# Feed-forward on four PSUM banks with the attention's tail and the narrow attention's head beside its products, and the wide attention's probability sums taken for four heads at once

## The reference

```python
# L0: 20 heads of 64 ("wide")
x = cross_attention(layer_norm(x, g1, be1), layer_norm(x, g1, be1), wq1, wk1, wv1, wo1, bo1) + x
x = cross_attention(layer_norm(x, g2, be2), context, wq2, wk2, wv2, wo2, bo2) + x
h = einsum('bne,ef->bnf', layer_norm(x, g3, be3), w1) + b1      # 320 -> 2 * 1280
a, gate = h[..., :1280], h[..., 1280:]
x = einsum('bnf,fe->bne', a * gelu(gate), w2) + b2 + x
# L1: the same block with 20 heads of 16 ("narrow") and the exact gelu
# L2: attention over 2 x 16 context tokens with two gates, + x
# L3: cross attention with 20 heads of 16, + x
# inside each attention
attn = softmax(q @ k.T * scale);  out = (attn @ v) @ wo + bo
```

## Time and profile before

| | |
|---|---|
| median of 3 runs | 3481.67 us (3481.03 to 3483.08) |
| the profiled execution, its own time | 3482.07 us |
| its span | 3480.3 us |
| granted TensorE clock, mean | 0.985 |
| PE busy | 3284.0 us (94%) |
| DVE, ACT, POOL busy | 1760.0 (51%), 1505.8 (43%), 672.0 (19%) us |
| the chain that ended last | PE 86%, ACT 6%, DVE 5%, issue 2% |

### The profile page before, as it was taken

The page is one execution under the profiler, slowest core; times in us unless marked ns, Lnnn a source line. Parts: engine busy times, 40 slices in busy tenths (PEclk is TensorE's granted clock), DMA queues, the critical chain, the costliest instruction groups (busy, mean ns, idle before and its releaser), DMA issues.

```text
span 3480.3 us, 39327 instructions
## 1 busy us (share of the span) xinstructions
PE 3284.0 (94%) x15478; PEld 1478.6 (42%) x15478; DVE 1760.0 (51%) x2728; ACT 1505.8 (43%) x2023; POOL 672.0 (19%) x420
## 2 busy tenths in 40 slices
PE   7999999999999999998999899999997999989997
PEld 3434344443434343434454344444433455643443
DVE  2645455454545455562223666777771221656774
ACT  3544444444454545451111555666652111326664
POOL 2433334333334343340000000000000000000000
PEclk9999999999999999999999999999999999989999
DMA  3000000000100000002000000000003000000000
GB/s 109 20 16 19 17 16 19 22 15 22 32 16 19 16 22 13 16 7 59 0 1 25 1 1 1 22 9 7 1 1 83 0 1 22 3 5 6 5 1 31
DMA packets 43558, 60.54 MB, mean 17 GB/s; under 512 B 7408, under 2 KB 31216, under 8 KB 43376
## 3 DMA queue, kind: packets, MB, share of 16 engines
q1 hardware_dynamic: 43376, 58.02, 5.8%
HBM read 55.39 MB, written 2.62 MB: 17 GB/s over the span
## 4 chain that ended last, share of the span: by engine, by line
PE 86%; ACT 6%; DVE 5%; issue 2%; DMA 0%; POOL 0%; SPq 0%; ACTq 0%; DVEq 0%; POOLq 0%
PE bank L548 8%; PE bank L465 8%; PE bank L1027 6%; PE bank L670 5%; PE bank L350 5%; PE bank L606 4%; PE bank L1463 4%; PE bank L960 4%; PE bank L1465 4%; PE bank L1143 3%; PE bank L609 3%; PE bank L642 3%; PE bank L1466 2%; PE bank L1080 2%; PE bank L1168 2%; DVE heads L985 2%
## 5 line engine op out<-in xcount | busy, mean ns | idle before, releaser
L498 DVE TENSOR_REDUCE heads<-bank 128x2 f32<-128x1024 f32 x320 | 392.4, 1226 | 673.7 <-PE bank L487 673.7
L985 DVE TENSOR_REDUCE heads<-bank 128x1 f32<-128x512 f32 x960 | 597.9, 683 | 237.2 <-PE bank L973 236.4
L521 ACT ACTIVATE probs<-bank 128x1024 f32<-128x1024 f32 x320 | 327.7, 1024 | 130.1 <-PE bank L474 129.9
L534 POOL TENSOR_TENSOR heads<-heads,probs 128x1024 f32<-128x1024 f32 x160 | 377.1, 2357 | 12.5
L530 POOL TENSOR_TENSOR heads<-probs 128x1024 f32<-128x1024 f32 x80 | 192.4, 2405 | 931.9 <-ACT probs L521 931.9
L465 PE MATMUL bank<-heads 64*128 64x512 f32 x1280 | 335.7, 602 | 0.1
L960 PE MATMUL bank<-heads 32*128 32x512 f32 x1920 | 296.5, 628 | 25.7 <-ACT weights L998 14.9
L548 PE MATMUL bank<-probs,values 128*64 128x512 f32 x1280 | 292.3, 598 | 9.3 <-ACT heads L617 4.9
L577 DVE RECIPROCAL rec<-ox 128x128 f32<-128x128 f32 x320 | 270.2, 907 | 8.0 <-ACT ox L570 8.0
L998 ACT ACTIVATE weights<-bank 128x1024 f32<-128x1024 f32 x238 | 230.6, 1021 | 100.2 <-PE bank L960 99.6
L1487 ACT ACTIVATE probs<-bank,b_col 128x512 f32<-128x512 f32 x80 | 55.0, 687 | 455.3 <-PE bank L1466 455.3
(11 more groups left out here) (199 smaller groups left out, 4725.2 us busy)
## 6 DMA issues: line engine op xcount, KB each, us to landing
heads<-in_wqk SPq DMA_DIRECT2D x40, 320.0 KB, 2.9
heads<-in_wqk SPq DMA_DIRECT2D x40, 256.0 KB, 2.6
ctx_in<-in_ctx SPq DMA_DIRECT2D x12, 384.0 KB, 3.7
weights<-in_L_xattn_wo SPq DMA_DIRECT2D x2, 1600.0 KB, 11.7
x_res<-in_x SPq DMA_DIRECT2D x4, 640.0 KB, 12.3
out<-x_res SPq DMA_DIRECT2D x1, 2560.0 KB, 8.7
weights<-in_L_xattn_w_ff SPq DMA_DIRECT2D x1, 1600.0 KB, 12.3
weights<-in_L_xattn_ff_w SPq DMA_DIRECT2D x1, 1600.0 KB, 14.2
```

Of the source, the lines that this page charges most:

```text
L498: nc.vector.tensor_reduce(v["negm"][:, U % 2, qb, :].rearrange("p (g k) -> p g k", g=2)[:, :, 0], M.ROWS[:, :, :], AX.X, ALU.max, negate=T ...
L521: nc.scalar.activation(v["probs"][:, kb, :, :], M.COLS[kb % 2][:, :, :], ACT.Exp, scale=float(r.work[n][0].prm["dh"]) ** -0.5).then_inc(r. ...
L534: nc.gpsimd.tensor_tensor(ps, ps, pr[:, k, :, :], ALU.add).then_inc(r.sem("part"), 1)
L985: nc.vector.tensor_reduce(v["negm"][:, tile, qb, 32 * h + at:32 * h + at + 1], r.bank_of(item, m)[:, :], AX.X, ALU.max, negate=True).then_ ...
```

## The change

1. *Wide run, denominators.* `den` is taken only in odd steps, for the pair of this step and the one before: four products with 32 columns of `ones` each instead of two with 64. The result has the four heads in four strips of 32 partitions. DVE takes four reciprocals per two steps (in the even step after), and ACT then spreads them: a copy of all 512 columns and four copies of 32 partitions, from strip to strip, to give one divisor for the even pair (`rec`) and one for the odd pair (`rec_odd`). DVE divides two pairs in the next odd step.
2. *Wide run, turns.* y moves from u = 1 to 4 to u = 2 to 5, V2 from u = 5 and 6 to u = 0 and 1. In the last batch u = 7 gets T0 to T2 of the feed-forward's first batch. The round after the last batch is gone: the y tiles of batch 7 stand behind the products j = 1 to 4 of the feed-forward.
3. *Feed-forward.* Gate in banks 2 and 3, linear half in 0 and 1, y in 0 and 1, input in 6 and 7. For odd j the pair on 64 rows comes first, ahead of the full products, so that the pairs of two j stand next to each other. The third input transposition moves behind the first tile of y. The weights come in two blocks in the order in which they are used, the first during the attention.
4. *Narrow run.* Its head stands between the pieces of the last batch's output product in s2 (`MEET`), its tail behind the products j = 0 to 3 of s5 (`TAIL`). Weight tiles and probability slots get other places in SBUF.

The core of the diff:

```diff
                 if u in (1, 2, 3, 4) and old:            # WideRun.step_items, wide_pe
-                    items += [(f"y{u - 1}", n - 1)]
+                if u in (2, 3, 4, 5) and old:
+                    items += [(f"y{u - 2}", n - 1)]
-                if u in (5, 6) and now:
-                    items += [(f"V2_{2 * u - 10}", n), (f"V2_{2 * u - 9}", n)]
+                if u in (0, 1) and now:
+                    items += [(f"V2_{2 * u}", n), (f"V2_{2 * u + 1}", n)]
...
-            for g in range(2):                           # w_den_pe
-                last = nc.tensor.matmul(r.bank_of(item, n)[64 * g:64 * g + 64, :], M.ones[:, :], v["psum"][:, U % 2, g, :], start=True, stop=True)
+            for e in range(2):
+                for g in range(2):
+                    at = 64 * g + 32 * e
+                    last = nc.tensor.matmul(r.bank_of(item, n)[at:at + 32, :], M.ones[:, 0:32], v["psum"][:, e, g, :], start=True, stop=True)
...
+        def w_spread_act(act, r, U):
+            odd = n_view(r, 0)["rec_odd"]
+            r.wait(act, "rcp", 4 * (U // 2 + 1))
+            nc.scalar.copy(odd[:, :], M.rec[:, :]).then_inc(r.sem("spread"), 1)
+            r.wait(act, "spread", 5 * (U // 2) + 1)
+            for a in (0, 64):
+                nc.scalar.copy(odd[a:a + 32, :], M.rec[a + 32:a + 64, :]).then_inc(r.sem("spread"), 1)
+            r.wait(act, "spread", 5 * (U // 2) + 3)
+            for a in (0, 64):
+                nc.scalar.copy(M.rec[a + 32:a + 64, :], M.rec[a:a + 32, :]).then_inc(r.sem("spread"), 1)
+
+        def w_divide_dve(dve, r, U):
+            r.wait(dve, "spread", 5 * (U // 2 + 1))
+            for W, rec in ((U - 1, M.rec), (U, n_view(r, 0)["rec_odd"])):
+                out = n_view(r, W // 10)["OT"][W % SLOTS]
+                r.wait_out(dve, f"mix{W % 10}", W // 10)
+                nc.vector.tensor_tensor(out, out, rec[:, :], ALU.mult).then_inc(r.sem("on"), 1)
...
+                    if u % 2 and 0 <= 10 * n + u - 2 < 10 * r.N:   # wide_act, behind the K cast
+                        w_spread_act(act, r, 10 * n + u - 2)
...
+                    if u % 2 == 0 and U >= 2:                      # wide_dve, behind the maxima
+                        w_recip_dve(dve, r, U - 1)
+                    if u % 2 and U >= 3:
+                        w_divide_dve(dve, r, U - 2)
+                    if u in (2, 3, 4, 5) and old:
+                        w_y_dve(dve, r, n - 1, u - 2)
...
+                    elif b > s.first:                              # ff_pe
+                        pe.wait_ge(s.sem("ysum"), after(b, TB, j - 1))
-                    gate, lin = M.ST[j % 2], M.PJ[j % 2]
+                    gate, lin = M.SM[j % 2], M.PJ[j % 2]
+                    if j % 2 == 0:
+                        ff_large(v, gate, j, 0, True)
+                        ff_large(v, lin, j, 1, True)
+                        ff_pair(v, gate, lin, j, False, s)
+                    else:
+                        ff_pair(v, gate, lin, j, True, s)
+                        ff_large(v, gate, j, 0, False).then_inc(s.sem("g_ps"), 1)
+                        ff_large(v, lin, j, 1, False).then_inc(s.sem("a_ps"), 1)
+                    if b == s.first and r.wide:
+                        wide_tail_pe(pe, r, j)                     # y tiles of batch 7 for j = 1 to 4
+                    elif b == s.first:
+                        narrow_steps_pe(pe, r, r.N, *ff_tail(r, j))
...
+        MEET = [(7, 7), (7, 7), (7, 11), (11, 14), (14, 15), (15, 16), (16, 17), (17, 20)]
+        TAIL = {0: (0, 3), 1: (3, 4), 2: (4, 7), 3: (7, 12)}
```

More of the change, by code:

```diff
@@ L157, in views @@
             if s.kind == "ff":
[L158 to L161, removed]
+                v["w1"] = M.weights[:, 3200:9600].rearrange("p (j c f) -> p j c f", j=10, c=5)
+                v["wo"] = M.weights[:, 0:3200].rearrange("p (c f) -> p c f", c=10)
+                v["OT"] = [M.mixed[:, c * N:c * N + N] for c in range(9, -1, -1)]
+                v["gate"] = M.ctx_in[:, :, :].rearrange("p (s t) d -> p s (t d)", s=2)
                 return v
@@ L453, in step_items @@
                 if now:
-                    items += [(f"mix{u}", n), (f"den{u}", n)]
+                    items += [(f"mix{u}", n)] + ([(f"den{u}", n)] if u % 2 else [])
                 return items
@@ L682, in w_T_pe @@
         def w_T_pe(pe, r, n, c):
-            (s, b), item, a = r.work[n], f"T{c}", 128 * c
+            item, a = f"T{c}", 128 * c
             r.wait_free(pe, item, n)
+            if n == r.N:
+                input_pe(pe, r.then, r.bank_of(item, n), c).then_inc(r.full(item, n), 1)
+                return
+            s, b = r.work[n]
             if c == 0:
@@ L922, in step_items @@
                     items += [("K2", n)]
-                if i == 3 and new:
+                feeds = new or now and self.then
+                if i == 3 and feeds:
                     items += [("T0", n + 1)]
@@ L1092, in T_pe4 @@
         def T_pe4(pe, r, n, c):
-            (s, b), item, (a, w) = r.work[n], f"T{c}", CH3[c]
+            item, (a, w) = f"T{c}", CH3[c]
             r.wait_free(pe, item, n)
+            if n == r.N:
+                input_pe(pe, r.then, r.bank_of(item, n), c).then_inc(r.full(item, n), 1)
+                return
+            s, b = r.work[n]
             if c == 0 and s.prm["ln"]:
@@ L1389, in narrow_pool @@
             ln = s0.prm["ln"]
-            start(pool, s0, s0.first)
+            if not r.led:
+                start(pool, s0, s0.first)
             for n in range(-1, r.N):
@@ L1470, in ff_pe @@
                 if b == s.first:
                     ff_weights(pe, s, "wo_in")
-                start(pe, s, b)
                 out_pe(pe, s, b)
         def ff_act(act, s):
-            v = V[s.name]
+            v, r = V[s.name], s.prev
+            for b in range(s.first, s.first + B):
+                if b > s.first:
+                    act.wait_ge(s.sem("a_ps"), after(b, NF, 0))
+                    inputs_act(act, s, b)
+                for j in range(NF):
+                    act.wait_ge(s.sem("g_ps"), after(b, NF, j + 1))
+                    if j == 0 and b == s.first:
+                        act.wait_ge(s.w_in, 16 * s.n_loads)
+                    if j >= 2 or b > s.first:
+                        act.wait_ge(s.sem("ot"), after(b, NF, j - 1))
+                    nc.scalar.activation(v["gate"][:, j % 2, :], M.SM[j % 2][:, :], s.prm["gelu"],
+                                         bias=M.b1_col[:, NF + j:NF + j + 1]).then_inc(s.sem("gelu"), 1)
+                    if b == s.first and not r.wide:
+                        narrow_steps_act(act, r, r.N, *ff_tail(r, j))
@@ L1477, in ff_act, with ff_dve @@
+            if s.follow:
+                narrow_steps_act(act, s.follow, -1, 0, 20)
+        def ff_dve(dve, s):
+            v, r = V[s.name], s.prev
             for b in range(s.first, s.first + B):
                 if b == s.first:
[L1479 to L1488 removed]
@@ L1490, in ff_dve @@
-        def ff_dve(dve, s):
-            v = V[s.name]
-            for b in range(s.first, s.first + B):
-                start(dve, s, b)
-                dve.wait_ge(s.w_in, 16 * s.n_loads)
+                    dve.wait_ge(s.w_in, 16 * s.n_loads)
+                if b == s.first and not r.wide:
+                    r.wait_full(dve, "mix4", r.N - 1)
+                if b + 1 == s.first + B and s.follow:
+                    narrow_begin_dve(dve, s.follow)
                 for j in range(NF):
```

662 lines of the change are left out of this document (368 added, 294 removed).

## The result

| | before | changed |
|---|---|---|
| median of 4 runs | 3481.35 us (3477.19 to 3483.08) | 3499.09 us (3497.37 to 3503.27) |
| ratio | | 1.0054, 95% interval 1.0037 to 1.0072 |
| the profiled execution, its span | 3480.3 us | 3495.6 us |
| granted TensorE clock, mean | 0.985 | 0.98 |

The account below looks back on a forecast made before the run. PE, busy 94% of the span, was taken as the bound; gains of 80.7 us are taken back by ACT's copies and the clock. Sum +2.6 us, 3484.7, on the median 3484.3; range for 8 in 10 3458 to 3503.

Parts of the forecast that it names:

- 1 denominators: Wide run: 40 of 80 dens go, -34.5 us; one more change of shape costs +3.8, bounds 0 and 7.6.
- 2 stalls behind the copies: Wide run, odd steps and u = 9: PE waits behind ACT's five copies, +58.1 us, bounds +12 and +66.
- 3 clock: Wide run: granted clock falls after ten of the stalls at 1.7 us each, +17.0 us, bounds 0 and 42.
- 4 feed-forward: Feed-forward: adjacent pairs save 40 double changes of shape, -15.1 us; waits between batches and s5's end, -1.7.
- 5 wide run to s2: Last den to j = 1 of s2 falls from 45.2 to 27.1 us; with 1 back for the clock, -17.1.
- 6 s4 to s5: Last mix to j = 1 of s5 falls from 30.85 to 17.2 us; with +1.3 in round 7, -12.3.
- 7 head of s3: Last gelu to first scores rises from 63.0 to 67.4 us, PE standing 15 us for weight loads: +4.4.
- the clock falls at every stall: Wide run, rival: falls at all 15 stalls cost 25.5 to 42 us, total 3493 to 3510, centre 3502; chance 0.22.
- two rivals: Wide-run clock: it holds after the stalls, 3468, chance 0.22; or falls at all 15, 3493 to 3510, chance 0.22.
- the forecast's own range: Whole kernel: 3475 to 3494 us for the forecast itself, from the small terms; the forecast's chance was 0.38.

Follow-up runs that it names:

- e7: e5 with two-head denominators in every step as in the kernel before, and no copies on ACT: 3428.74 us, ratio 0.9849.
- e1: Changed kernel with ACT's five copies moved behind their step's evacuations and DVE's two divisions behind the add of y: 3423.92 us, ratio 0.9839.
- e3: Changed kernel with extra products of unread result ahead of negm in PE's stalls at u = 7 and u = 1: 3479.30 us, ratio 0.9994.
- e4: Changed kernel with the q, k and v loads of s3 issued after six of ten tiles instead of all ten: 3479.93 us, ratio 0.9998.
- e6: e5 with every feed-forward tile's pair on 64 rows last, so no two pairs stand next to each other: 3419.37 us, ratio 0.9820.
- e8: Changed kernel without the four 32-partition copies, so most heads are divided by something else: 3426.98 us, ratio 0.9842.
- e2: Changed kernel with ACT's copies moved as in e1 but DVE's divisions kept ahead of the add of y: 3528.17 us, ratio 1.0139.
- e5: Changed kernel with e1's copies move, e4's earlier loads, and DVE's divisions behind the layer norm too: 3401.27 us, ratio 0.9768.

## Why the prediction was right, and where it was off

By its own steps, in us (forecast, then measured):

| step | forecast | measured | from |
|---|---|---|---|
| 1 denominators | -34.5 + 3.8 | -29.2 | even steps 0.86 shorter, odd ones 0.14 longer, 40 pairs; e7: 27.5 |
| 2 stalls behind the copies | +58.1, 2.8 of it T work | +58.4, and 2.8 of T work | idle on PE; e1 takes them away |
| 3 clock | +17.0 | +23.7 | e3; 13 falls, not 10; e4's trace 24.1 |
| 4 feed-forward | -15.1 - 1.7 | -15.2 - 2.5 | 1.9 per batch; e6: 18.1 |
| 5 wide run to s2 | -17.1 | -18.8 | 53.4 later than before at the last den, 32.7 at the last gelu of the first batch of s2, less one batch's 1.9 |
| 6 s4 to s5 | -12.3 | -15.2 | 40.1 later in s4's last batch (1.2 of it new there), 21.8 at the last gelu of the first batch of s5, less 1.9 |
| 7 head of s3 | +4.4 | +11.9 | 62.9 to 74.8 from gelu to scores; without the wait (e4) 19.2 less |

- Step 2 was right in kind and nearly in size. The choice between bounds of 12 and 66 was made by the rows of 618 and 599 ns, and e8 shows it: without the four small copies 72 us go. The single stalls were each a little off: 3.89 for u = 7 against my 3.55, 3.01 for u = 1 in cross attention, 0.4 to 0.7 at the steps with y. One set of copies delays T0 by 3.2 us and not by 2.87, which makes 26.4 us at u = 7 instead of 23.0; 1.8 less at the steps with y hides about half of that. That the sum comes so close is partly luck.
- Steps 3 and 7 were mis-sized most, by 6.7 and 7.5 us, both upward; steps 1 and 2 add 4.6, and steps 4 to 6 give 5.5 back. That makes +15.9 out of +2.6. In step 3 I had a fall at 7 of 8 steps with T and at 3 of 7 with V2, at 1.7 each; it was 8 and 5, at 1.5 and 2.3. My rival "the clock falls at every stall" was nearer. In this trace it fell at 3.0 us in four of four batches, and at 2.3 and 2.6 in one of three: at two equal stalls of 2.30 us, in batches 1 and 2, it held once and fell once. In e4's trace of the same instructions it fell at 3.0 us in two of four, and at none of 2.3 and 2.6. The Trainium skill says in "TensorE: Matmul & The Clock Gate", Part 1, that the moment of a change varies from run to run; the two traces agree.
- A reading that step 3 and two rivals lean on does not hold: that the 2.93 us wait for POOL alone left the clock alone. In the kernel before, PE worked for about a microsecond behind that wait and then stood still again, and 2.5 us after the den's start the clock was down, early in the second idle time, so that row can't tell the two apart. The same wait stands at the end of the wide run in every kernel, 2.57 to 2.93 us long. With work following at once the clock fell within 1.4 us of the den's start in five traces of nine (e2, e4, e5, e6, e8) and held in four. In e8 the products behind it took 5.40 us, where they take 3.70 in the changed kernel:

```profile
1549.54 1.06 PE L594 MATMUL bank<-heads,ones 128*32 128x512 f32 x8 [2.92 <-POOL heads L562]
1550.53 5.40 PE L1564 MATMUL bank<-hT,weights 128*128 128x512 f32 x8
```

- Step 1: the saving came out smaller, since an odd step is 0.14 us longer than before (mix to den and back to the row products costs more with 32 columns), 5.6 us in all. I had put 3.8 for this change of shape. By the page "TensorEngine Tiling (Array Packing)", Tiling Modes, of the Trainium skill, each change of tiling mode drains the engine. The 0.14 would fit such a price, below the 0.19 that I had as the upper bound, but no run here shows a drain as such. The four products do run side by side: eight records in 1.06 us.
- Step 7: the stall was 16.28 against 15 forecast. The other 6 us I had missed: Q0 at half speed and other low stretches, about 3 (in e4 Q0 to first scores takes 44.5 us, here 47.5), about 2 more of short waits in the head (an estimate, what is left over), and 1.5 that are no loss, since the last gelu is now ahead of the last products.
- Step 6 came out better: before, the first products of s5 ran at the low clock, which that step did not count. The stretch in the kernel before (ten us around the first products), then the one in the changed kernel:

```profile
2651.00:2661.00 10.00, 6.42 (x11) 2.96 (x12) 0.00 (x0) 3.31 (x4) 0.00 (x0) 0.52 0.95 260
```

```profile
2640.00:2672.00 32.00, 22.05 (x145) 6.35 (x138) 7.32 (x14) 17.15 (x19) 0.00 (x0) 0.89 0.15 52
```

The measured column sums to 15.9; with 1.3 less for an earlier first score and 1.7 more in s7, which stays unexplained, that is 16.3, where the spans differ by 15.3. What I did not weigh enough is that the clock and the head can err together: PE stood still for ACT and for loads, and both times it lost clock too. The range held because it reached to the rival's centre; the forecast's own range did not hold. e3's two falls at u = 9 are not the work of its extra products, since e4 has three there without them. Left open: what decides whether one of these stalls brings a fall, and the 0.5 per batch in e6.

## What to carry to other kernels

Before work is added to an engine that looks half idle, look at which of its instructions another engine waits for, and put the new ones behind those, at a place where it waits itself; the same five copies cost 75 us more at one place than at another, where they were hidden with 0.2 us to spare. Move all engines of such a chain together: the copies without the divisions made it worse. And when PE comes to wait at many places, count its clock as a second price: here 23.7 us on 58.4 us of added waiting, and some 30 on 77 in e2. Price it over the whole run and not stall by stall, since the same stall paid in one execution and not in the next.

## What the runs showed of the hardware

A copy on ACT of 32 partitions by 512 columns took 0.62 us, the same as 128 partitions.

The length of a single wait did not decide alone whether the granted clock fell. Over the wide run of the changed kernel, traced twice (its own trace and e4's), it fell at 16 of 16 waits of 3.89 us, at 6 of 8 of 3.01, at none of two of 2.58 and at one of four of 2.30. In e2 it fell at all 14 waits of 5.5 us. It also fell where no wait was over 1.22 us: in three steps u = 9 of e4 and two of e3, and once of eight times behind 1.19 us in e8. In e1, with waits of at most 1.42 us before the last den, it did not fall at all. In the changed kernel a fall cost 0.8 to 3.0 us, most where full-length products followed. PE products whose result nobody uses were worth 20 us for that reason alone.
